# Picks in twos: four VectorE operations over two neighbouring banks of scores instead of eight over one

## What is computed

```
L0 (T = 2048 tokens, H = 512):
  approx_up = x @ up_w.T;  delta = x @ gate_w.T - local_point
  attn = approx_up @ out.T + sum over m = 1..6 of (terms of |delta|^m * approx_up) @ fuse_m.T
  ffn  = silu(x @ ffn_gate_w.T) * (x @ ffn_up_w.T) @ ffn_down_w.T        (F = 1248)
  x1   = layernorm(x + attn + ffn)
sparse part (INTER = 1792, blocks of 32, RANK = 16):
  inter = x1 @ c1_w.T @ c2_w.T                    # the scores, 1792 for each token
  blk   = inter.reshape(B * T, 56, 32)
  idx   = argmax(blk, axis=-1) + arange(0, 1792, 32)
  h     = relu(x1 . w1[idx]);  out = sum over the 56 blocks of h * w2t[idx]
  result = layernorm(x1 + out)
```

## Time and profile before

| | us |
|---|---|
| three runs | 715.2, 715.85, 715.96 |
| their median | 715.85 |
| profiled execution, its own time | 715.6 |
| its span, first to last instruction | 713.8 |
| mean granted TensorE clock | 0.998 of full speed |
| busy: TensorE, VectorE, ScalarE, GpSimd | 704.0, 527.3, 269.2, 290.8 |

### The profile page before, as it was taken

How to read it: one execution, slowest core, us unless ns; L and a number is a source line. 1 busy time by engine, 2 the same in 40 slices (tenths; PEclk the granted TensorE clock), 3 DMA queues, 4 the chain that set the end, 5 groups by cost and what they waited for, 6 DMA issues and landing times.

```text
span 713.8 us, 10308 instructions
## 1 busy us (share of the span) xinstructions
PE 704.0 (99%) x3949; PEld 380.2 (53%) x3949; DVE 527.3 (74%) x977; ACT 269.2 (38%) x455; POOL 290.8 (41%) x276
## 2 busy tenths in 40 slices
PE   8999999999999999999999999999999999999996
PEld 3444444444444444444444456666666666667763
DVE  5979897796887778677786988958885778337235
ACT  1565457444812121221222234444334333443342
POOL 0452452211111151244314576897356435643331
PEclk9999999999999999999999999999999999999999
DMA  9637309401000110111020222131222101220101
GB/s 324 265 116 224 59 7 357 109 6 53 2 15 17 22 22 2 27 27 20 6 16 19 50 50 50 25 69 16 50 74 64 47 4 60 61 45 1 60 2 60
DMA packets 40833, 44.67 MB, mean 63 GB/s; under 512 B 25296, under 2 KB 33104, under 8 KB 39888
## 3 DMA queue, kind: packets, MB, share of 16 engines
q1 hardware_dynamic: 37808, 39.29, 18.5%
q0 software_dynamic: 2112, 4.19, 3.5%
q10 hardware_dynamic: 864, 0.53, 0.2%
HBM read 34.33 MB, written 4.42 MB: 54 GB/s over the span
## 4 chain that ended last, share of the span: by engine, by line
PE 85%; issue 1%; DVE 1%; ACT 1%; POOL 1%; DVEq 0%; ACTq 0%
PE acc L547 31%; PE pb L527 15%; PE pa L527 15%; PE pb L784 10%; PE pa L784 8%; PE acc L624 2%; PE acc L873 2%; PE pick_a L690 1%; PE pick_b L690 1%; POOL big L1154 1%; PE pick_a L675 0%; ACT work L1116 0%; PE pick_b L873 0%; PE pick_b L543 0%; PE acc L543 0%
## 5 line engine op out<-in xcount | busy, mean ns | idle before, releaser
L547 PE MATMUL acc<-big,work 128*128 128x512 f16 x1038 | 235.1, 379 | 0.0
L1147 POOL TENSOR_TENSOR work<-work 128x512 f16<-128x512 f32 x90 | 107.5, 1206 | 273.5 <-ACT work L1019 213.7
L547 PEld LDWEIGHTS acc<-big,work 128*128 128x128 f16 x1038 | 101.6, 98 | 115.4
L527 PE MATMUL pa<-xs,big 128*128 128x512 f16 x480 | 111.2, 379 | 0.0
L527 PE MATMUL pb<-xs,big 128*128 128x512 f16 x480 | 110.1, 379 | 0.0
L1876 DVE TENSOR_TENSOR pa<-pa,big 128x512 f32<-128x512 f32 x28 | 19.6, 699 | 79.7 <-ACT big L1099 68.7
L527 PEld LDWEIGHTS pa<-xs,big 128*128 128x128 f16 x480 | 46.1, 98 | 54.0
L527 PEld LDWEIGHTS pb<-xs,big 128*128 128x128 f16 x480 | 46.1, 98 | 53.4
L624 PE MATMUL acc<-big 128*128 128x512 f16 x336 | 73.8, 379 | 0.6 <-DVE big L1466 0.4
L1019 ACT ACTIVATE work<-work 128x512 f16<-128x512 f32 x40 | 25.2, 630 | 111.0 <-DVE work L1603 111.0
L1154 POOL TENSOR_TENSOR big<-work,big 128x512 f16<-128x512 f32 x27 | 36.7, 1375 | 64.2 <-ACT big L955 63.9
(11 more groups left out here) (225 smaller groups left out, 983.0 us busy)
## 6 DMA issues: line engine op xcount, KB each, us to landing
big<-in_w_all SPq DMA_DIRECT2D x2, 3840.0 KB, 17.5
big<-in_x_t SPq DMA_DIRECT2D x16, 256.0 KB, 7.9
rows<-in_x POOLq DMA_DIRECT2D x4, 1024.0 KB, 13.4
big<-spread_rows SPq DMA_DIRECT2D x16, 256.0 KB, 6.1
big<-in_w_all SPq DMA_DIRECT2D x2, 1536.0 KB, 11.9
big<-spread_rows SPq DMA_DIRECT2D x16, 192.0 KB, 5.1
out<-rows SPq DMA_DIRECT2D x3, 1024.0 KB, 4.4
big<-in_w_all SPq DMA_DIRECT2D x1, 2048.0 KB, 15.1
```

The lines of the kernel that those rows point to most:

```text
L527: mm = nc.tensor.matmul(dst[:, :], weights(wp)(kc * P, P), x_part16(g, xp, kc), start=(kc == 0 and wp == xp), stop=(kc == KC - 1 and wp == 1))
L547: mm = nc.tensor.matmul(acc[t][:, :], act_part(pair, j, ap, t * P, P), weights(wp)(0, H), start=(first and ap == wp), stop=(last and ap == 1))
L1147: nc.gpsimd.tensor_tensor(act_part(pair, j, 1), act32[j], act_part(pair, j, 0), ALU.subtract).then_inc(act_lo, halves)
```

## The change

`pick_a` and `pick_b` become the two halves of one PSUM tensor of 1024 columns, `pick_banks`; the marks, the ranks and the block maxima become tensors of two halves as well. `find_hits` and `rank_hits` take n picks (1 or 2) from bank k % 2 on; with n = 2 each of the four operations runs over both banks, 2 x 448 columns. `find_hits` then waits for n scores and raises `score_used` by n. In a unit of stage 1 the calls are now: picks 0 and 1 together before the second `swiglu`, picks 2 and 3 together after it (pick 2 stood before it). In the units without a next tile, pick 2 alone stays before the second `swiglu` and pick 3 alone in the next unit. In stage 2 both picks of a unit are one call, and `low_first` stands ahead of it.

```diff
-        pa, pb, pick_a, pick_b = bank("pa"), bank("pb"), bank("pick_a"), bank("pick_b")
+        pa, pb = bank("pa"), bank("pb")
+        pick_banks = ctx.enter_context(nc.psum_tensor("pick_banks", [P, 1024], F32))
+        pick_a, pick_b = pick_banks[:, 0:512], pick_banks[:, 512:1024]
...
+            def find_hits(tile, k, n=1):
+
+                at, q = slice(k % 2, k % 2 + n), tile * PICKS + k
+                scored = in_blocks(pick_banks[:, :].rearrange("p (a c) -> p a c", a=2)[:, at, 0:PICK_COLS])
+                best = block_max[:, at, :]
+                dve.wait_ge(score_ready, q + n)
+                step(v.tensor_reduce(best, scored, axis=AX.X, op=ALU.max))
+                settle()
+                v.tensor_tensor(in_blocks(hit[:, at, :]), scored, best.unsqueeze(3).broadcast_to([P, n, PB, SPARSITY]),
+                                ALU.is_equal).then_inc(score_used, n)
+
+            def rank_hits(tile, k, n=1):
+
+                at, q = slice(k % 2, k % 2 + n), tile * PICKS + k
+                dve.wait_ge(score_used, PICKS + q + n)
+                step(v.tensor_tensor(rank[:, at, :], hit[:, at, :], rev_wide[:, :].unsqueeze(1).broadcast_to([P, n, PICK_COLS]), ALU.mult))
+                settle()
+                won = winner[:, bass.ds((tile % 2) * P + k * PB, n * PB)].rearrange("p (a b) -> p a b", a=n)
+                last = v.tensor_reduce(won, in_blocks(rank[:, at, :]), axis=AX.X, op=ALU.max)
...
-                pick(tile, 0, pick_a)
-                pick(tile, 1, pick_b)
-                pick(tile, 2, pick_a)
+                pick(tile, 0, 2)
+                if nxt is None:
+                    pick(tile, 2)
                 swiglu(g, u, 1)
                 if nxt is not None:
-                    find_hits(tile, 3, pick_b)
+                    find_hits(tile, 2, 2)
                     if g * U1 + u in JOB_IN_SWIGLU and g * U1 + u < GROUPS * U1 - 1:
                         cut_z(nxt, pick_a)
-                    rank_hits(tile, 3)
+                    rank_hits(tile, 2, 2)
...
-                    pick(tile, k, pick_a)
                     if n in LOW_BY_DVE:
                         low_first(n)
-                    pick(tile, k + 1, pick_b)
+                    pick(tile, k, 2)
```

More of the change, by code:

```diff
@@ L236, in program @@
         z_stack = big16[:, a16 + 512:a16 + 640].bitcast(BF16)
-        hit = [big16[:, a16 + 640 + i * PICK_COLS:a16 + 640 + (i + 1) * PICK_COLS] for i in range(2)]
-        rank = [big16[:, a16 + 1536 + i * PICK_COLS:a16 + 1536 + (i + 1) * PICK_COLS] for i in range(2)]
-        block_max = [words(a32 + H + 1216 + i * 16, PB) for i in range(2)]
+        hit = big16[:, a16 + 640:a16 + 640 + 2 * PICK_COLS].rearrange("p (a c) -> p a c", a=2)
+        rank = big16[:, a16 + 1536:a16 + 1536 + 2 * PICK_COLS].rearrange("p (a c) -> p a c", a=2)
+        block_max = words(a32 + H + 1216, 2 * 16).rearrange("p (a b) -> p a b", a=2)[:, :, 0:PB]
         winner = big16[:, a16 + 2496:a16 + 2496 + 2 * P]
@@ L284, in bank @@
             return ctx.enter_context(nc.psum_tensor(name, [P, 512], F32))
-        pa, pb, pick_a, pick_b = bank("pa"), bank("pb"), bank("pick_a"), bank("pick_b")
+        pa, pb = bank("pa"), bank("pb")
+        pick_banks = ctx.enter_context(nc.psum_tensor("pick_banks", [P, 1024], F32))
+        pick_a, pick_b = pick_banks[:, 0:512], pick_banks[:, 512:1024]
         acc = [bank(f"acc{t}") for t in range(TPG)]
-        pick_bank = [pick_a, pick_b]
         HALF = H // 2
@@ L1716, in cut_z @@
                 v.tensor_tensor(pieces(6, 2), wide(z_rest, 2), pieces(3, 2), ALU.subtract).then_inc(z_cut, 1)
[L1718 to L1725, removed]
-                settle()
-                v.tensor_tensor(h, s, block_max[b].unsqueeze(2).broadcast_to([P, PB, SPARSITY]), ALU.is_equal).then_inc(score_used, 1)
@@ L1729, in rank_hits, with in_blocks @@
[L1729 to L1736, removed]
+            def in_blocks(a):
+                return a.rearrange("p a (b j) -> p a b j", j=SPARSITY)
@@ L1737, in rank_hits @@
+            def rank_hits(tile, k, n=1):
+                at, q = slice(k % 2, k % 2 + n), tile * PICKS + k
+                dve.wait_ge(score_used, PICKS + q + n)
+                step(v.tensor_tensor(rank[:, at, :], hit[:, at, :], rev_wide[:, :].unsqueeze(1).broadcast_to([P, n, PICK_COLS]), ALU.mult))
                 settle()
-                last = v.tensor_reduce(winner[:, bass.ds((tile % 2) * P + k * PB, PB)], r, axis=AX.X, op=ALU.max)
-                if k == PICKS - 1:
+                won = winner[:, bass.ds((tile % 2) * P + k * PB, n * PB)].rearrange("p (a b) -> p a b", a=n)
+                last = v.tensor_reduce(won, in_blocks(rank[:, at, :]), axis=AX.X, op=ALU.max)
+                if k + n == PICKS:
@@ L1742, in rank_hits, with pick @@
                     step(last)
-            def pick(tile, k, src):
-                find_hits(tile, k, src)
-                rank_hits(tile, k)
+            def pick(tile, k, n=1):
+                find_hits(tile, k, n)
+                rank_hits(tile, k, n)
             def w2_low(c0, c1):
@@ L1842, in first_unit1 @@
                 if last is not None:
-                    pick(last, 3, pick_b)
+                    pick(last, 3)
             def tile_units1(g):
```

## The result

| | before | after |
|---|---|---|
| median, runs side by side | 715.59 us (12 runs, 715.2 to 716.19) | 717.41 us (12 runs, 717.11 to 717.75) |
| ratio, 95% interval | | 1.0024 [1.0017, 1.0032] |
| span of the profiled execution | 713.8 | 715.7 |
| VectorE busy | 527.3 | 507.4 |

The forecast was 716.3 and "same" with 0.79. The time lies in the range, 1.1 us over the forecast. By the prediction's own bound of 0.2% it stands on the edge: 1.8 of 715.6 us are 0.25%, and the interval of the ratio goes from 0.17 to 0.32%. But it is a loss clear of zero, 1.8 us where the sum had 0.4.

What follows compares the result with a forecast made beforehand. TensorE, busy 704.0 of 713.8 us, was taken as the bound. Median 715.85 plus 0.4 us of waits at score 2 gave 716.25, stated as 716.3; everything else counted nothing. Range 715.2 to 717.9.

Steps and rivals of the forecast that it cites:

- bad ends of tiles 9 and 10: Stage 1: the picks of these tiles might begin 1.12 us after score 0, not 0.81, costing 0.3 us more each.
- Worth of VectorE's time: Whole kernel: merged pairs save 18 us of VectorE's 527, beside a TensorE that does not wait, so worth nothing.
- Price of the doubled operations: VectorE, merged picks: reduction 1.08 us, compare and last reduction 1.09 each, ranking multiplication 0.62.
- The rival that two banks cost double: Each two-bank operation costs what two do now: 0.31 us more per find in nine tiles, 719.05 us; chance 0.13.
- the lost fast mode of the ranking: Doubled ranking takes 1.09 us, not 0.62, delaying three tiles by 0.47 each: 717.65 us; chance 0.05.
- Where the find begins: Stage 1, nine tiles: the pick begins 0.73 us after score 0 in six, 0.81 in tiles 5, 9 and 10.
- The find against score 2: Stage 1, nine tiles: score 2 waits until both banks are compared; 6 x 0.015 + 3 x 0.10 = 0.4 us.
- dead heat: Stage 1, tile 0: score 2 could start at 222.15 and is due at 222.14, a wait of 0.00 to 0.03 us.
- Stage 2 at nothing: Stage 2, ten merged calls: nothing on TensorE waits for their scores for most of a unit; cost nothing.
- The wait would have to pass 2.4 us: Stage 2, unit 5: VectorE's wait for ScalarE's conversion moves nothing below this, given 1.76 us idle and 0.63 saved.
- The port rival: VectorE and GpSimd share a port: a doubled ranking blocks GpSimd 0.24 us longer, no TensorE wait hangs on it; no chance given.
- Slower: Two rivals, two banks not one access (0.13) and ranking losing its fast mode (0.05); chance together 0.18.

Runs made afterwards that it cites:

- before_no_rank: Kernel before the change with the ranking multiplication left out: 715.38 us against 715.48 us, ratio 0.9998.
- inc_one: Changed kernel, but a find of two banks raises score_used by one and the waits count finds: 717.14 us against 715.53 us before the change.
- find_each: Changed kernel with reductions and compares bank by bank, only ranking and last reduction over two banks: 715.62 us against 715.53 us before the change.
- all_mended: Changed kernel: finds raise score_used by one, stage 1's first find precedes x1's low part, tile 12's picks single with low part between in unit 5: 715.96 us.

## Where the prediction held and where it failed, step by step

The time came within the range, but the loss is over four times the 0.4 of the sum, and that it stayed in the range is partly luck: the upper end was drawn for the bad ends of tiles 9 and 10 and a slow ranking, which did not come, and two other costs took their room.

- **Worth of VectorE's time: right.** 20 us fewer (18 forecast) buy nothing, as before_no_rank shows in another way.
- **Price of the doubled operations: right.** 1.08, 1.09 and 0.62 us as forecast. The rival that two banks cost double is out; so is the lost fast mode of the ranking. The Trainium skill (VectorE: DVE Perf Modes, on the TRN2 errata) gives 1.06 as an estimate, and the find would have been 0.05 shorter; the traces have 1.077 and 1.092, so the measurement decides against it.
- **Where the find begins: right.** 0.73 after score 0 in six tiles, 0.80 in tiles 5, 9 and 10 (forecast 0.81). Tile 10's bad end of 1.12 did not come.
- **The find against score 2: mis-sized.** The failed step is "The compare starts 0.64 + 0.47 later". It starts 1.18 later, since raising the semaphore by two takes the wait out of the instruction. 0.07 us in a dead heat counted in full nine times: the term measured 1.07 us where 0.4 was forecast. With the 0.07 taken out (inc_one) it measured 0.39. The dead heat itself was read rightly. What was left out is that the changed increment, not only the changed width, is part of the operation.
- **Stage 2 at nothing: wrong.** It cost 0.70 us. The failed sentence is "nothing on TensorE waits for them for most of a unit". The z product of tile 13 waits for pick 2 of tile 12 in the unit behind it, with 0.64 us to spare before the change. The slack was measured for the z product of stage 1 (2.1 us) and not for those of stage 2. The last sentence of the forecast named this wait as a way to be wrong, and late masks as another; both came.
- **"The wait would have to pass 2.4 us": beside the point.** VectorE did not come late to its mask by its own queue; it still idled 1.30 us. GpSimd did, which the low part and the ranking had slowed, and its last operation (L1236) is what releases the mask. The port rival said that "no TensorE wait hangs on" GpSimd; one did, through the mask, by up to 0.37 us.
- **Rivals.** "Slower" was put on two mechanisms that did not happen, and the two that did were in neither. The first of them was said to decide "from the point where a find lasts over 2.25 us": the find did last 2.27, but by the wait ahead of the compare and not by the price of two banks. The two misses, 0.67 and 0.70, are 1.37 us; with the forecast's 0.4 that makes 1.77 of the measured 1.82.

What is not settled: why a stream of VectorE stumbles at those places (only that moving it by two instructions removes the delay is shown), and why GpSimd's work of unit 5 begins 0.09 us late. The 0.05 to 0.07 us behind the z product of tile 13 go with that by their size, which no run tests.

## What to carry to other kernels

Merging two operations makes each cheaper and their first result later: before merging, list every buffer that the merged operation releases, and for each waiter write down how much earlier than needed its release comes today. Where that slack is about as large as the merged operation's extra length, merge the part behind the release and leave the part ahead of it single (here find_each, which still lost 0.3 of the 1.9 us by the trace). And follow the chain through engines that share something with the doubled operation, not through its own queue alone.

## What the runs showed of the hardware

- An instruction of VectorE that raises a semaphore by two stood behind a semaphore instruction of its own (21 ns) and began 0.103 to 0.105 us after its predecessor's end, in all 30 places; raising by one (inc_one) it carried its wait and began 0.034 to 0.035 after.
- One VectorE operation over two neighbouring PSUM banks costs per element what it costs within one: the reduction took 0.610 us for 448 elements and 1.077 for 896, 1.04 ns for each more, beside 1.05 from the rows of one bank.
- Where an operation of VectorE and one of GpSimd met, one or both took longer: GpSimd's small sums 1.05 to 1.17 us instead of 0.73 to 0.76, the doubled ranking at 497.88 1.24 instead of 0.62.
- Right behind a semaphore instruction, places 703, 831 and 959 of VectorE's stream began 0.40 us late in eight of thirteen executions; where it fell into the tail of the kernel (all_mended, inc_one) it cost TensorE 0.36 us. So edits of half a microsecond can be swamped by where instructions fall, and two empty instructions took that wait away.
- Waits of 0.10 to 0.16 us of TensorE's matmuls do not appear in its list of waits; a row of the weight load names the place, not the size. The spacing of the matmuls' starts shows them, and nine of them made more than half of the loss.
